# A buffer of queries laid out block by block instead of interleaved, in a split-precision attention and feed-forward layer

## The reference, cut to what matters

```python
x  = L0_attn_x                                # (2, 1024, 256), float32
xn = layernorm(x)
out = x + attn(xn) + ffn(xn)

def attn(x):                                  # 16 heads of 128, causal
    q = (x @ Wq + bq).reshape(b, h, t, dh)    # a plain reshape, no transpose
    k = (x @ Wk + bk).reshape(b, t, h, dh).transpose(0, 2, 3, 1)
    v = (x @ Wv + bv).reshape(b, t, h, dh).transpose(0, 2, 1, 3)
    w = softmax(q @ k / sqrt(128) + causal_mask)
    return (w @ v).transpose(0, 2, 1, 3).reshape(b, t, h * dh) @ Wo + bo
# ffn(x): gate, up and down projections with 4-bit weights that are decoded first, gelu(gate) * up
```

## Time and profile before

| | us |
|---|---|
| median of 3 runs | 1334.18 (1333.24 to 1334.37) |
| the profiled execution | 1334.87 |
| its span, first to last instruction | 1333.0 |

### The profile page before, as it was taken

The page is one execution under the profiler, slowest core; times in us unless marked ns, Lnnn a source line. Parts: engine busy times, 40 slices in busy tenths (PEclk is TensorE's granted clock), DMA queues, the critical chain, the costliest instruction groups (busy, mean ns, idle before and its releaser), DMA issues.

```text
span 1333.0 us, 21111 instructions
## 1 busy us (share of the span) xinstructions
PE 1255.8 (94%) x7724; PEld 1078.5 (81%) x7724; DVE 946.2 (71%) x1478; ACT 758.2 (57%) x1575; POOL 794.4 (60%) x797
## 2 busy tenths in 40 slices
PE   3799999999899999999999999999999999999997
PEld 2677777777678888878888887888888878888886
DVE  7777887788766666676666677767666776676666
ACT  3565556555356566635666564456665536566652
POOL 5666666666356657634766664366766536666662
PEclk9899999999999999999999999999999999999998
DMA  4000000010200000020000001000000100000021
GB/s 93 12 13 13 13 11 8 12 32 0 79 28 13 25 5 21 13 66 15 21 13 13 25 5 58 27 25 5 20 13 17 45 24 13 17 21 5 5 64 67
DMA packets 60986, 32.45 MB, mean 24 GB/s; under 512 B 17120, under 2 KB 60896, under 8 KB 60896
## 3 DMA queue, kind: packets, MB, share of 16 engines
q1 hardware_dynamic: 59280, 29.99, 8.0%
q10 hardware_dynamic: 1616, 1.25, 0.3%
HBM read 29.12 MB, written 2.10 MB: 23 GB/s over the span
## 4 chain that ended last, share of the span: by engine, by line
PE 63%; DVE 5%; ACT 4%; issue 1%; POOL 0%; ACTq 0%
PE ps L43 18%; PE ps L44 18%; PE ps L45 17%; PE ps L1074 9%; DVE o_lo L915 2%; DVE v_lo L870 1%; ACT v_hi L719 1%; ACT o_hi L755 1%; PE ps L1063 1%; ACT pt_hi L748 1%; DVE q_all L898 1%; ACT probs L762 1%; DVE neg_max L953 1%; DVE pt_lo L910 0%; DVE wq_lo L883 0%
## 5 line engine op out<-in xcount | busy, mean ns | idle before, releaser
L910 DVE TENSOR_TENSOR pt_lo<-ps,pt_hi 128x512 fp32r<-128x512 f32 (+3 forms) x384 | 203.8, 552 | 222.7 <-ACT pt_hi L748 218.9
L839 POOL TENSOR_TENSOR inv_sum<-row_sum,minus_one 128x1 f32<-128x1 f32 x256 | 141.5, 553 | 307.7 <-ACT probs L762 307.4
L842 POOL TENSOR_TENSOR probs<-probs,inv_sum 128x128 f32<-128x128 f32 (+7 forms) x256 | 296.3, 1158 | 20.0
L762 ACT ACTIVATE probs<-ps,neg_max 128x128 f32<-128x128 f32 (+7 forms) x256 | 189.7, 741 | 146.5 <-DVE neg_max L953 143.1
L748 ACT ACTIVATE pt_hi<-ps 128x512 fp32r<-128x512 f32 (+3 forms) x384 | 174.2, 490 | 104.4 <-PE ps L1074 104.4
L953 DVE TENSOR_REDUCE neg_max<-ps 128x1 f32<-128x128 f32 (+7 forms) x256 | 192.0, 750 | 9.8 <-PE ps L1063 3.5
L44 PE MATMUL ps<-pt_lo,v_hi 128*128 128x256 f32 (+1 forms) x640 | 177.3, 277 | 0.0
L45 PE MATMUL ps<-pt_hi,v_lo 128*128 128x256 f32 (+1 forms) x640 | 176.8, 276 | 0.0
L1074 PE MATMUL ps<-ident,probs 128*128 128x128 f32 x1152 | 171.2, 276 | 3.5 <-DVE pt_lo L910 1.4
L43 PE MATMUL ps<-pt_hi,v_hi 128*128 128x256 f32 (+1 forms) x640 | 173.5, 271 | 0.7 <-DVE pt_lo L910 0.7
L43 PE MATMUL ps<-k_hi,q_hi 128*128 128x512 f32 (+3 forms) x384 | 140.6, 366 | 5.3 <-ACT probs L762 3.4
(11 more groups left out here) (108 smaller groups left out, 3079.2 us busy)
## 6 DMA issues: line engine op xcount, KB each, us to landing
wq_in<-in_wq SPq DMA_DIRECT2D x64, 128.0 KB, 2.3
kv_in<-in_wk SPq DMA_DIRECT2D x16, 256.0 KB, 2.6
vw_in<-in_wv SPq DMA_DIRECT2D x32, 128.0 KB, 2.3
wo_in<-in_wo SPq DMA_DIRECT2D x32, 128.0 KB, 2.0
q_all<-in_x SPq DMA_DIRECT2D x1, 2048.0 KB, 9.4
out<-q_all SPq DMA_DIRECT2D x8, 256.0 KB, 2.2
raw<-in_gate SPq DMA_DIRECT2D x18, 64.0 KB, 1.8
raw<-in_up SPq DMA_DIRECT2D x18, 64.0 KB, 2.0
```

Source lines behind the costliest of these rows:

```text
L762: nc.scalar.activation(probs[:, s % 4, 0:width], flat(S[place[("S", *divmod(s, TILES))] % 2])[:, 0:width], ACT.Exp, bias=neg_max[:, s % 16 ...
L839: nc.gpsimd.tensor_tensor(inv_sum[:, at], row_sum[:, at], minus_one[:], ALU.pow).then_inc(inv_done, 1)
L842: nc.gpsimd.tensor_tensor(row, row, inv_sum[:, at].to_broadcast([P, (i + 1) * P]), ALU.mult).then_inc(probs_done, 1)
L910: nc.vector.tensor_tensor(pt_lo[where], T[at % 2][:, 0:blocks * P].rearrange("p (a b) -> p a b", b=P), pt_hi[where].bitcast(F32), ALU.subt ...
```

## The change

The axes of `q_all` are put in another order: [partition, column block c, head m, token row r]. L898 then writes one c for all (m, r) as 512 elements in a row. `q_split` and `q_low` read the same 512 elements in the same order as before, row r outside and block c inside, so their reads now step 512 elements (2048 bytes) from one element to the next, 16 times, and then start over one element on. What they write (`q_hi`, `q_lo`) and `q_low`'s second operand (`q_hi`) lie as before. `x_res` is the same number of bytes at the start of the buffer. No instruction, wait or DMA is added, removed or moved.

```diff
-        q_all = sb("q_all", [P, GROUP, SEQ // HEADS, HEADS], F32)
+        q_all = sb("q_all", [P, HEADS, GROUP, SEQ // HEADS], F32)
...
-        x_res = q_all[:, 0:NT * DM // SEQ].rearrange("p a r c -> p (a r c)")
+        x_res = q_all[:, 0:NT * DM // N].rearrange("p c m r -> p (c m r)")
...
             def q_split(h, half):
 
-                rows = q_all[:, h % GROUP, half * 32:half * 32 + 32, :].rearrange("p r c -> p (r c)")
-                nc.scalar.activation(q_hi[:, half, :], rows, ACT.Copy).then_inc(q_hi_done, 1)
+                rows = q_all[:, :, h % GROUP, half * 32:half * 32 + 32].rearrange("p c r -> p r c")
+                nc.scalar.activation(q_hi[:, half, :].rearrange("p (r c) -> p r c", c=HEADS), rows, ACT.Copy
+                                     ).then_inc(q_hi_done, 1)
...
             def q_low(h, half):
-                rows = q_all[:, h % GROUP, half * 32:half * 32 + 32, :].rearrange("p r c -> p (r c)")
-                low(q_lo[:, half, :], rows, q_hi[:, half, :], q_hi_done, 2 * h + half + 1, q_lo_done)
+                rows = q_all[:, :, h % GROUP, half * 32:half * 32 + 32].rearrange("p c r -> p r c")
+                lo, hi = (t[:, half, :].rearrange("p (r c) -> p r c", c=HEADS) for t in (q_lo, q_hi))
+                low(lo, rows, hi, q_hi_done, 2 * h + half + 1, q_lo_done)
...
                     dve.wait_ge(qp_done, o * HEADS + n + 1)
-                    dst = q_all[:].rearrange("p m r c -> p (m r) c")[:, :, n:n + 1]
                     nc.vector.tensor_scalar(
-                        dst.rearrange("p a b -> p (a b)"), S[place[("Q", o, u)] % 2][:, v, :], bq[:, n:n + 1],
+                        q_all[:, n, :, :].rearrange("p m r -> p (m r)"), S[place[("Q", o, u)] % 2][:, v, :], bq[:, n:n + 1],
                         SCALE, ALU.add, ALU.mult).then_inc(q_done, 1)
```

## The result

The changed kernel is slower: 1340.02 us (median of 5 runs, 1338.78 to 1340.80) against 1333.97 (5 runs, 1332.88 to 1334.37) for the kernel before on the same chip. The ratio is 1.0044 (95% interval 1.0033 to 1.0056), so +6.0 us. Its profiled execution took 1340.8, with a span of 1338.8, 5.8 more than before. The source is a few lines longer now. L748, L762, L824, L898, L910 and L1074 of before are one line further on here (L749, L763 and so on), L865 is L867 and L877 is L879.

A forecast was written before the change was run, and what follows sets the result against it. TensorE was taken to bound the kernel, so only changes to its gaps count. 0.52 + 0.65 + 4.05 + 0.4 - 0.75 = +4.9 us on 1334.18 gave 1339.1; 8 in 10 range 1332.8 to 1350.

The forecast's parts named there:

- nearer to the second: ScalarE's strided read gains 0.44 us, between 0.35 (write's penalty) and 0.47 (a hop allows one word per 1.74 ns for any engine).
- Between the 0.35 and the 0.47: GpSimd's q_lo gains 0.43 us, between 0.68 ns more an element and the common hop rate; bounds 0 and 1.28.
- Start: 345 to 379 us, chain to the first scores: -0.35 for the write, +0.44 q_hi, +0.43 q_lo, so +0.52 us.
- Head 0: q_hi of half 1 delays `exps` of tile 1, and GpSimd's tiles come late behind it: +0.65 us.
- Ordinary heads: Step 5: longer q_hi delays pt_hi, pt_lo, evacuation and TensorE's Vb; beyond 0.29 us slack, 27 x 0.15 = 4.05 us.
- step 1 of odd heads: pt_hi of tile 7 and pt_lo come late for the transposes: d - 0.41 = 0.03 us in 12 heads, 0.4.
- GpSimd in ordinary heads: Probabilities of tile 6 in even heads have 0.9 us of slack against q_lo's 0.43: no cost; odd heads have more.
- Rival C: GpSimd becomes the late engine with a q_lo that doubles: +9.6 us, 1343.8; chance 0.10.
- Rival D: VectorE's relief shows, which needs TensorE to wait for L898 in bulk; chance 0.06 together with the unforeseen.
- Query groups: Inside heads 7, 15 and 23 VectorE's shorter write shortens TensorE's gaps: 3 x 0.25, -0.75 us.
- Rival A: Strided reads cost little (d up to 0.3): 1333.1 us if free, about 1334.8 at 0.3; chance 0.27.
- Rival B: ScalarE's read pays more than the strided write did, at the bound d = 0.80: +19.6 us, 1353.8; chance 0.15.

The follow-up runs named there:

- both variants with an extra copy: Kernel before plus a contiguous ScalarE copy behind q_hi in step 5: 128 elements, 1334.29 us, ratio 1.0000; 512 elements, 1339.57 us, ratio 1.0044.
- ScalarE only: Kernel after with GpSimd's q_low read made contiguous, ScalarE's read still strided: 1340.95 us against 1334.06 for the kernel before, ratio 1.0048.
- reordered: Kernel after with ScalarE doing pt_high of tile 3 before q_split in steps 5 and 6: 1335.63 us against 1334.06 for the kernel before, ratio 1.0013.
- the GpSimd experiment: Kernel after with ScalarE's q_split read made contiguous, GpSimd's read still strided: 1333.20 us, ratio 0.9996 to the kernel before.
- the pairs: Kernel after with blocks kept in twos: VectorE writes every second word, readers take runs of two; 1333.42 us against 1334.29 before, ratio 0.9992.

## Why the prediction held, point by point

1339.1 was forecast for 1334.18, +4.9; +6.0 came out (+5.8 in the profiled spans; the interval of the ratio is 4.4 to 7.5 us and holds both).

- *L898*: 745 forecast, 747 measured.
- *L725*: +0.44 forecast. The record grew by 0.50. What the next instruction sees is the distance from q_hi's start to its own: to pt_hi's 0.60 before and 1.02 after (0.42 more), to the probabilities' in head 0 0.52 and 0.96 (0.44 more). Both numbers are the same event; the distance is what enters the sum. Per element it is (1118 - 197) / 512 = 1.80 ns with the 197 ns of fixed cost of the earlier trace rows, near the 1.74 of VectorE's write. So on these two engines single words come at about the same rate, which is what "nearer to the second" rested on. It is no rule for all engines: q_lo, in the next bullet, does not follow it.
- *q_lo*: +0.43 forecast, +0.27 measured, the one wrong price. "Between the 0.35 and the 0.47" was the step that failed. The read went from 2.12 to 2.65 ns an element, 0.53 more, less than the 0.68 of VectorE's write, and neither hidden under 2.12 ns nor the difference to a common rate. Why it is 0.53 stays open. The error does little harm, since in the traces only the first gap sees it. The Trainium skill (GPSIMD Engine Reference, "Performance pitfalls for Q7 kernels") has half as much again for such a read, 1.92 us by the prediction's estimate. Here the subtraction with one of two inputs strided took 1.55, 21% more, so the rule is too high for it.
- *Start*: +0.52 forecast, +0.38 measured. By the starts of the rows, the write gave back 0.32 (0.35 forecast), the ScalarE read cost 0.46 (0.44) and q_lo 0.24 (0.43). The shortfall is q_lo's.
- *Head 0*: +0.65 forecast. The gap grew by 0.88 (0.61 to 1.49), but half of that is not the change: with the clock at full speed up to the gap it is 1.04 with both reads contiguous and 1.49 with ScalarE's strided. From the start of k_hi to the released scores it is 1.71 us in before, in the variant with both reads contiguous and in both variants with an extra copy, and 2.16 to 2.18 wherever q_hi is strided and ahead (after, ScalarE only, reordered): +0.45. With the 0.09 behind it, 0.54.
- *Ordinary heads*: 4.05 + 0.4 forecast, 4.42 in the trace. Of 0.12 at Vb (0.15 forecast) 27 times make 3.2, and the step 1 of odd heads turned out dearer: 0.07 for 0.03, 12 times 0.8. Those two and a drift of 0.01 to 0.02 in a head are the 4.42. So the total is nearer to the forecast than its two terms, of which one was too high and the other too low: that much is luck. Of the two signs named, the period came (54.46 for the 54.4 forecast), and the wait put down to DVE did not show as a wait. The row of after that answers to the last of the earlier trace rows comes 0.12 behind the mask ahead of it (705.45), where it came 0.06 behind it:

```profile
705.57 0.30 PE L1075 MATMUL ps<-ident,probs 128*128 128x128 f32 x1
```

- *GpSimd in ordinary heads*: nothing forecast, nothing found, and the GpSimd experiment confirms it. Rival C is out. Rival D is out by the experiment with both reads contiguous.
- *Query groups*: -0.75 forecast, -0.67 in the trace. The third wait of each group fell by 0.17 to 0.21 (0.18 forecast); around the second it is 0.04 (0.07 forecast), although that wait itself grew from 0.96 to 1.04. In ratios this gain is too small to see.
- *What the sum left out*: 0.31 of the first block, 0.41 of the clock at head 0 and 0.40 at the end. Without these 1.1 us the trace gives +4.7 for the 4.9 forecast. The change has no instruction in the first block. At the end the same work takes longer or shorter by the clock alone: from head 31 on, after and the reordered kernel run the same instructions, and from its first scores to the start of the last matmul they take 43.28 and 41.69 us. Whether the longer gap ahead of head 0 makes the clock fall more often is not shown by any run.

Rival A (reads that cost nothing) fell to L725's 1118 ns. Its deciding point, d = 0.29, is supported by the extra copies (0.26). Rival B's 0.80 was far off.

## What to carry to other kernels

Price a layout by who stands idle at each end. Here 19.5 us of work were taken from an engine that had them to spare, and 0.4 us added on another engine ahead of a hand-over with 0.3 us of slack, repeated 27 times, made over half of the loss (3.2 of 5.8 us). Before moving a stride from a writer to its readers, read the reader's queue for what stands behind it. An order that lets the short urgent copy go first got back about three quarters of the loss without shortening anything; the same move in another place passed the wait on to the next engine and made another one behind it.

## What the runs showed of the hardware

**Strides in SBUF, 512 fp32 elements a partition.** VectorE's write: 747 ns contiguous, 748 with a step of 8 bytes, 1125 with 16, 1094 with 64. ScalarE's read: 622 contiguous, 1118 for single words 2048 bytes apart, 665 for runs of two words, 621 for runs of four. GpSimd's: 1281, 1551, 1293. Every second word was written at full rate, which only one of the three theories for the pairs had. For the write two words in each 16 bytes were enough, one was not. The Trainium skill (SBUF — State Buffer, "Specifications (TRN2)") says that its 16-byte lines need at least two hits for full bandwidth; by that rule the write at 8 bytes is free and the one at 16 is not, and these runs agree (748 and 1125 ns).

**The granted clock behind the first gap.** It was 0.50 (the 1.2 GHz level) for some microseconds after a gap of 1.91 us in before. This is the kernel after, behind its gap of 2.29 us:

```profile
380.00:381.00 1.00, 1.00 (x7) 0.91 (x6) 0.29 (x1) 0.33 (x2) 0.00 (x0) 0.50 0.00 0
```

The length of the gap alone does not order it. At this place it fell after 1.90, 1.91 and 2.29 us (the two extra-copy runs, before, after, the reordered ones), and stayed at 1.00 after 1.58, 1.62, 1.83, 1.96 and even 2.04 (ScalarE only). Near the end, between 1308 and 1317 us, all twelve traces have the same gap of 1.91 us. Behind it the clock fell to 0.50 for about 3 us in six of them and stayed at 1.00 in the other six, before among these. First scores to k_hi take 2.54 to 2.56 us at full clock and 3.68 to 4.12 after a fall, so it is worth 1.1 to 1.6 us. The first figure of the prediction on this, 1.2 us, was about right. It makes two profiled spans that differ by a microsecond no evidence of anything. Ratios over many runs are evidence, and so is a stretch in which the clock stays at 1.00. From the first scores of head 1 to those of head 31 it does in all twelve: before takes 887.12 us, both reads contiguous 886.32, GpSimd's alone strided 886.33, ScalarE's alone 891.34, after 890.96.
